# Preparing q, k and v in an attention kernel: the lower parts moved from GpSimd to VectorE, v's bias added by TensorE

## The chip, the cores and the metric

The kernel runs on one core of a Trainium2 chip. The metric is the time on the device of one execution in microseconds (us), lower is better. Engine names are short in the profile: PE is TensorE, PEld its weight loads, DVE is VectorE, ACT is ScalarE, POOL is GpSimd, SP is SyncE.

## What is computed

One transformer layer over 32 sequences of 256 tokens with 128 channels, in float32. The first half is attention with 8 heads:

```python
xn = (x - mu) * rsqrt(var + eps) * gamma + beta      # of an x that was normalised once before
q = xn @ Wq + bq ; k = xn @ Wk + bk                  # 8 heads of 16
v = xn @ Wv + bv                                     # 8 heads of 128
p = softmax(q k^T / 4) ; out = sum over 8 neighbours of (p v)
x = x + out
```

The second half is a mixture of 8 experts with a top-2 choice, `x = x + sum over 2 experts of gate * (gelu(u @ W1 + b1) @ W2 + b2)`, with u the normalised x. The change touches q, k and v only.

Since the output of attention is summed over groups of 8 channels of v, the kernel sums the columns of Wv and bv in such groups once, at the start (`Wv_s`, `bv_s`), and v is then 16 wide for each head.

## The kernel before

Every engine has its own program, written out by hand in the order in which it runs; semaphores (`wait(engine, semaphore, count)`, `.then_inc(...)`) tie them together. Attention is a software pipeline of **periods**, one for each of the 32 sequences (`batch`), with a few before and after. A period of PE has 8 units k = 0 to 7. Unit k holds `max_unit` (L821: two products for the scores' row maxima, of this period's sequence) and `st_unit` (L833: two products for the transposed scores, of the sequence two periods back). Both write PSUM tiles of which there are two, so `max_unit` k waits until DVE has reduced unit k - 2 (`reduce_unit`, L1032), and `st_unit` k until ACT has taken the exponential of unit k - 2 (L682). The products of probabilities and v (`av`, L851) follow at k = 2 and k = 7.

Two sequences form a **pair**, whose normalisation and projections are made together: x is normalised by DVE, POOL and ACT into `z`, transposed by PE and scaled by ACT to `xnT`, and multiplied by Wq at k = 5 of an odd period (L907), by Wk at k = 2 of the next even one (L880), and by `Wv_s` at k = 4 of the even period after that (L931, four products of 128 columns). q and k go through one PSUM tile, `ps_proj`.

The scores need more exactness than one fast product gives, so q and k are each split in a high part (rounded to the type F32R) and a low part, the rest. Before the change this goes as follows for q (k alike, L739, L740 and L554):

```python
act.activation(q_f32[:], ps_proj[:], ACT.Identity, bias=bq_c[:, 0:1])
act.activation(q_hi[par][:], ps_proj[:], ACT.Identity, bias=bq_c[:, 0:1]).then_inc(q_hi_ready, 1)
...
pool.tensor_tensor(lo[par][:], x[:], hi[par][:].bitcast(F32), ALU.subtract).then_inc(lo_ready, 1)
```

ACT copies the projection twice out of PSUM, and POOL subtracts. SP then spreads the parts over `q_stack` and `k_stack` with six DMAs for each sequence (L408), a period before they are needed. v leaves PSUM by DVE (L1173, at k = 6), which adds `bv_s` on the way into `v_aug`.

POOL has a program of its own order in each period (`body` in its block): statistics of the next pair (L578), four indirect DMAs that scatter the rows of `y` to the experts' slots (L590, from period 9 on; each takes POOL's time to issue), the lower part of k (even periods) , the attention output's division and its addition to x (L600, L605), the lower part of q (odd periods), `rstd2` and `shift2` of the second normalisation (L614, L616) for which ACT's copies `y_row` wait (L711), and a piece of splitting the experts' weights (L566, L569). After period 27 DVE builds a table for the experts, and the expert half, with the last periods mixed into it, follows from about 370 us.

## Time and profile before

| what | value |
|---|---|
| median of 3 runs | 707.14 us (706.84 to 707.73) |
| the profiled execution, its own time | 707.2 us |
| its span from first to last instruction | 705.4 us |
| busy: PE, PEld, DVE, ACT, POOL | 578.7, 440.5, 523.7, 486.6, 494.2 us |
| mean granted TensorE clock | 0.937 of full speed |
| share of the chain that ended last: PE, POOL, issue, DMA, DVE, ACT | 38, 20, 9, 6, 6, 4% |

Busy times are sums over engines that work side by side. The chain that ended last follows the work back from the last instruction, at each step to what released it. A timeline shows an engine's instructions with start and length; lengths of neighbours overlap where an engine is pipelined, so what an instruction costs its engine is the distance to the next start. In brackets behind a row stands the engine's idle time before it and what ended that.

### The profile page before, as it was taken

The numbers are of one execution on the slowest core, as the hardware profiler recorded it, in microseconds if no ns is written. First come the engines' busy times: TensorE is split into PE (matmuls) and PEld (weight loads), VectorE is DVE, ScalarE is ACT, GpSimd is POOL, SyncE is SP. The second block draws the span as 40 slices with busy tenths as digits, with TensorE's granted clock in tenths as the row PEclk, the third lists the DMA queues.
The fourth block names the chain that finished last, engine by engine and source line by source line (L and its number), as shares of the span: only waits on it lengthen the run. The fifth ranks groups of instructions, "written<-read, shape, count | busy, mean of one in ns | idle before, by whom it ended". The sixth has DMA issues, their size and how long they took to land.

```text
span 705.4 us, 14432 instructions
## 1 busy us (share of the span) xinstructions
PE 578.7 (82%) x3889; PEld 440.5 (62%) x3889; DVE 523.7 (74%) x1557; ACT 486.6 (69%) x904; POOL 494.2 (70%) x571
## 2 busy tenths in 40 slices
PE   3799998988988989869976888689999999999200
PEld 1566766666666666636644666468888888888200
DVE  7578898988898888888852688457777777777274
ACT  3467878787777787755665887478888888888000
POOL 6434557888888888857886567757788788877700
PEclk9999999999999999979995899899999999999755
DMA  4645545554545645444325567998777778786099
GB/s 118 176 97 153 151 123 159 164 157 136 143 138 162 169 131 155 121 119 121 108 64 163 162 207 212 258 247 263 243 221 246 244 217 246 250 252 198 12 389 324
DMA packets 107570, 127.31 MB, mean 180 GB/s; under 512 B 19950, under 2 KB 86010, under 8 KB 106497
## 3 DMA queue, kind: packets, MB, share of 16 engines
q1 hardware_dynamic: 89600, 105.34, 51.4%
q0 software_dynamic: 9088, 16.94, 7.3%
q10 hardware_dynamic: 8832, 4.46, 2.1%
q8 instruction: 21, 0.34, 0.2%
q14 instruction: 29, 0.23, 0.1%
HBM read 69.26 MB, written 33.72 MB: 146 GB/s over the span
## 4 chain that ended last, share of the span: by engine, by line
PE 38%; POOL 20%; issue 9%; DMA 6%; DVE 6%; ACT 4%; SPq 2%; POOLq 0%; ACTq 0%; DVEq 0%
POOL slots L590 9%; PE ps_max L948 4%; PE ps_max L949 4%; PE ps_max L950 4%; DMA probs<-comb 3%; DMA probs<-slots 3%; PE ps_proj L1001 2%; PE ps_route L993 2%; PE ps_st L948 2%; PE ps_st L949 2%; PE ps_st L950 2%; PE ps_av L851 2%; PE ps_st L833 2%; PE ps_max L821 2%; POOL att_n L600 2%
## 5 line engine op out<-in xcount | busy, mean ns | idle before, releaser
L657 POOL DMA_INDIRECT comb<-probs,gate_row x156 | 179.8, 1152 | 42.9 <-issue 38.9
L1032 DVE TENSOR_REDUCE row_max<-ps_max 128x2 f32<-128x512 f32 x256 | 173.9, 688 | 47.4 <-PE ps_max L821 42.9
L682 ACT ACTIVATE probs<-ps_st 128x512 f32<-128x512 f32 x256 | 146.8, 594 | 57.6 <-PE ps_st L833 55.3
L1257 DVE TENSOR_TENSOR k_stack<-probs,k_stack 128x512 fp32r<-128x512 f32 x156 | 108.1, 693 | 75.1 <-ACT k_stack L783 73.0
L590 POOL DMA_INDIRECT slots<-y_row,slot_idx x128 | 125.5, 980 | 39.2 <-issue 37.6
L821 PE MATMUL ps_max<-k_stack,q_stack 96*128 96x256 f32 x512 | 132.6, 344 | 24.0 <-DVE row_max L1032 22.9
L821 PEld LDWEIGHTS ps_max<-k_stack,q_stack 96*128 96x128 f32 x512 | 81.8, 198 | 71.9 <-DVE row_max L1032 47.0
L833 PE MATMUL ps_st<-q_stack,k_stack 128*128 128x256 f32 x512 | 106.6, 291 | 13.2 <-ACT probs L682 12.8
L833 PEld LDWEIGHTS ps_st<-q_stack,k_stack 128*128 128x128 f32 x512 | 79.6, 192 | 21.3 <-ACT probs L682 19.1
L851 PE MATMUL ps_av<-probs,v_aug 128*32 128x256 f32 x1024 | 70.3, 393 | 0.0
L780 ACT ACTIVATE probs<-ps_st,b_cur 128x512 f32<-128x512 f32 x78 | 53.9, 692 | 23.1 <-DMA b_cur<-b_all 17.5
L948 PE MATMUL ps_max<-k_stack,q_stack 128*128 128x512 f32 x156 | 61.8, 396 | 0.0
L949 PE MATMUL ps_max<-k_stack,q_stack 128*128 128x512 f32 x156 | 61.5, 394 | 0.0
L950 PE MATMUL ps_max<-k_stack,q_stack 128*128 128x512 f32 x156 | 61.4, 394 | 0.0
L783 ACT ACTIVATE k_stack<-ps_st,b_cur 128x512 fp32r<-128x512 f32 x78 | 53.5, 687 | 0.0
L711 ACT ACTIVATE y_row<-X,shift,rstd 128x128 f32<-128x128 f32 (+1 forms) x64 | 27.7, 483 | 25.8 <-POOL shift L616 19.5
L780 ACT ACTIVATE probs<-ps_mv,b_cur 128x512 f32<-128x512 f32 x39 | 26.9, 691 | 21.5 <-PE ps_mv L950 21.0
L851 PEld LDWEIGHTS ps_av<-probs,v_aug 128*32 128x32 f32 x1024 | 27.1, 110 | 19.9 <-issue 1.9
L600 POOL TENSOR_TENSOR att_n<-att,rden 128x256 f32<-128x256 f32 x32 | 21.0, 657 | 22.5 <-DVE rden L1140 22.2
L948 PE MATMUL ps_st<-q_stack 128*128 128x512 f32 x78 | 35.2, 451 | 1.5 <-DVE q_stack L1257 1.5
L1257 DVE TENSOR_TENSOR q_stack<-ps_proj,q_stack 128x512 fp32r<-128x512 f32 x39 | 26.7, 685 | 11.8 <-ACT q_stack L792 11.8
L1001 PE MATMUL ps_proj<-ident,probs 128*128 128x128 f32 x156 | 25.5, 289 | 10.4 <-DMA probs<-slots 10.4
(175 smaller groups left out, 1275.2 us busy)
## 6 DMA issues: line engine op xcount, KB each, us to landing
q_stack<-w_split SPq DMA_DIRECT2D x78, 512.0 KB, 4.3
probs<-slots SPq DMA_DIRECT2D x39, 260.0 KB
q_stack<-q_hi SPq DMA_DIRECT2D x64, 128.0 KB, 2.7
k_stack<-k_hi SPq DMA_DIRECT2D x64, 128.0 KB, 3.0
probs<-comb SPq DMA_DIRECT2D x8, 1024.0 KB, 7.8
X<-in_L_attn_x_dram SPq DMA_DIRECT2D x16, 256.0 KB, 3.3
q_stack<-q_lo SPq DMA_DIRECT2D x32, 128.0 KB, 2.7
k_stack<-k_lo SPq DMA_DIRECT2D x32, 128.0 KB, 3.0
```

What stands on the lines that cost most here:

```text
L590: pool.indirect_dma_start(slots, bass.IndirectOffsetOnAxis(slot_idx[par_s][:, k, c:c + 1], 0), y_row[par_s][k][:, c, :], None).then_inc(sc ...
L657: pool.indirect_dma_start(comb_rows, bass.IndirectOffsetOnAxis(gate_row[r][:, c, 1:2].bitcast(I32), 0), res[r][:, c * P:(c + 1) * P], None ...
L682: act.activation(probs[slot % 2][:, h, :, :], ps_st[h % 2][:], ACT.Exp, scale=DK ** -0.5).then_inc(exp_done, 1)
L780: act.activation(h_f32[f % 2], ps_h[f], ACT.Gelu, bias=b_cur[r][:, f:f + 1]).then_inc(h_f32_ready, 1)
L821: last = pe.matmul(ps_max[k % 2][:, hh, :], q_stack[slot][0:M_ROW, h, sc * P:(sc + 1) * P], k_stack[slot][0:M_ROW, h, :], start=True, stop ...
L833: last = pe.matmul(ps_st[h % 2][:, tc, :], k_stack[slot][:, h, tc * P:(tc + 1) * P], q_stack[slot][:, h, :], start=True, stop=True)
L851: last = pe.matmul(ps_av[32 * j:32 * j + 32, g, :], v_aug[(slot // 2) % 2][:, 2 * (slot % 2) + tc, h, :], probs[slot % 2][:, h, tc, :], st ...
L948: pe.matmul(o, w_hi, x_hi, start=start, stop=False)
L949: pe.matmul(o, w_lo, x_hi, start=False, stop=False)
L950: return pe.matmul(o, w_hi, x_lo, start=False, stop=stop)
L1032: dve.tensor_reduce(row_max[slot % 2][:, sc, 2 * hp:2 * hp + 2], ps_max[k % 2][:], AX.X, ALU.max).then_inc(smax_reduced, 1)
L1257: dve.tensor_tensor(lo, x, hi.bitcast(F32), ALU.subtract).then_inc(s, 1)
```

## The change

ACT no longer writes `q_f32` and `k_f32`. DVE makes the lower parts from PSUM, with one instruction (`proj_lo`): (ps_proj + bias) - high part; for k behind the reduction of unit 4 of an even period, for q behind that of unit 7 of an odd one. POOL's two subtractions go. `ps_proj` is now free only when DVE has read it, so PE's next writers wait for the lower part too. For v, PE first multiplies a row of 128 ones by `bv_s`, repeated four times to 512 columns, and adds the four products with `Wv_s` onto it in PSUM; ACT instead of DVE copies v out, at unit 6.

```diff
             def set_v_and_route():
+                pool.memset(ones_row[:], 1.0).then_inc(v_rest_ready, 1)
...
-                if not t.odd and t.pair(2):
-                    n, par = t.pair(2)
-                    lo_part(n, par, k_f32, k_hi, k_lo, k_hi_ready, k_lo_ready)
...
-                if t.odd and t.pair(3):
-                    n, par = t.pair(3)
-                    lo_part(n, par, q_f32, q_hi, q_lo, q_hi_ready, q_lo_ready)
...
-                        wait(act, k_lo_ready, n)
-                        act.activation(k_f32[:], ps_proj[:], ACT.Identity, bias=bk_c[:, 0:1])
                         act.activation(k_hi[par][:], ps_proj[:], ACT.Identity, bias=bk_c[:, 0:1]).then_inc(k_hi_ready, 1)
...
-                        wait(act, q_lo_ready, n)
-                        act.activation(q_f32[:], ps_proj[:], ACT.Identity, bias=bq_c[:, 0:1])
                         act.activation(q_hi[par][:], ps_proj[:], ACT.Identity, bias=bq_c[:, 0:1]).then_inc(q_hi_ready, 1)
+                    if h == 6 and prep_v:
+                        n, par = prep_v
+                        wait(act, v_proj, n + 1)
+                        wait(act, av_done, 4 * n - 4)
+                        act.activation(v_aug[par][:, :, :, 0:DK], ps_mv[:].rearrange("p (c h d) -> p c h d", c=4, h=H),
+                                       ACT.Copy).then_inc(v_ready, 1)
...
                         wait(pe, q_hi_ready, n + 1)
+                        wait(pe, q_lo_ready, n + 1)
                         pe.matmul(ps_proj[:], Wk_p[:], xnT[par][:], start=True, stop=True).then_inc(k_proj, 1)
...
                         wait(pe, k_hi_ready, n)
+                        wait(pe, k_lo_ready, n)
...
+                        pe.matmul(ps_mv[:], ones_row[:], bv_s[0:1, :].unsqueeze(1).to_broadcast([1, 4, D]), start=True, stop=False)
                         for c in range(4):
                             last = pe.matmul(ps_mv[:, c * P:(c + 1) * P], xnT[par][:, c * P:(c + 1) * P], Wv_s[:],
-                                             start=True, stop=True)
+                                             start=False, stop=(c == 3))
...
+            def proj_lo(n, par, bias, hi, lo, hi_ready, lo_ready):
+
+                wait(dve, hi_ready, n + 1)
+                dve.scalar_tensor_tensor(out=lo[par][:], in0=ps_proj[:], scalar=bias[:, 0:1], in1=hi[par][:].bitcast(F32),
+                                         op0=ALU.add, op1=ALU.subtract).then_inc(lo_ready, 1)
...
+                    if k == 4 and prep_k:
+                        n, par = prep_k
+                        proj_lo(n, par, bk_c, k_hi, k_lo, k_hi_ready, k_lo_ready)
+                    if k == 7 and prep_q:
+                        n, par = prep_q
+                        proj_lo(n, par, bq_c, q_hi, q_lo, q_hi_ready, q_lo_ready)
...
-                    if k == 6 and prep_v:
-                        n, par = prep_v
-                        wait(dve, v_proj, n + 1)
-                        wait(dve, av_done, 4 * n - 4)
-                        dve.tensor_tensor(v_aug[par][:, :, :, 0:DK],
-                                          ps_mv[:].rearrange("p (c h d) -> p c h d", c=4, h=H),
-                                          bv_s[:].rearrange("p (o h d) -> p o h d", o=1, h=H).to_broadcast([P, 4, H, DK]),
-                                          ALU.add).then_inc(v_ready, 1)
```

Three places of the order, by engine. First DVE in an even period, before the change, from the transposition of the attention output at unit 4 to unit 6:

```order
L1136 STREAM_TRANSPOSE att<-ps_av 128x512
L1088 TENSOR_TENSOR y_row_0<-top,gate_rcp 128x4
L1089 TENSOR_SCALAR y_row_0<-token 128x4
L1088 TENSOR_TENSOR y_row_1<-top,gate_rcp 128x4
L1089 TENSOR_SCALAR y_row_1<-token 128x4
L1032 TENSOR_REDUCE row_max<-ps_max 128x2
L1140 RECIPROCAL rden<-att 128x16
L1093 TENSOR_TENSOR token<-token,token_step 128x4
L1095 TENSOR_TENSOR slot_sel<-slot_all,chosen 128x32 x2
L1032 TENSOR_REDUCE row_max<-ps_max 128x2
L1173 TENSOR_TENSOR v_aug<-ps_mv,bv_s 128x32x16
L1103 TENSOR_REDUCE slot_idx<-slot_sel 128x4 x2
```

and the same place now (line numbers are those of the changed kernel):

```order
L1140 STREAM_TRANSPOSE att<-ps_av 128x512
L1035 SCALAR_TENSOR_TENSOR k_lo<-ps_proj,bk_c,k_hi 128x512
L1091 TENSOR_TENSOR y_row_0<-top,gate_rcp 128x4
L1092 TENSOR_SCALAR y_row_0<-token 128x4
L1091 TENSOR_TENSOR y_row_1<-top,gate_rcp 128x4
L1092 TENSOR_SCALAR y_row_1<-token 128x4
L1029 TENSOR_REDUCE row_max<-ps_max 128x2
L1144 RECIPROCAL rden<-att 128x16
L1096 TENSOR_TENSOR token<-token,token_step 128x4
L1098 TENSOR_TENSOR slot_sel<-slot_all,chosen 128x32 x2
L1029 TENSOR_REDUCE row_max<-ps_max 128x2
L1106 TENSOR_REDUCE slot_idx<-slot_sel 128x4 x2
```

The instruction for k's lower part stands ahead of the reduction of unit 5; the one for v, behind the reduction of unit 6, is gone.

Second DVE at the end of an odd period, before:

```order
L1059 MAX_INDEX top_e<-top,sig 128x8 x4
L1032 TENSOR_REDUCE row_max<-ps_max 128x2
L1064 TENSOR_TENSOR chosen<-expert_n,top_e 128x32 x2
L1032 TENSOR_REDUCE row_max<-ps_max 128x2
L1032 TENSOR_REDUCE row_max<-ps_max 128x2
```

and now:

```order
L1062 MAX_INDEX top_e<-top,sig 128x8 x4
L1029 TENSOR_REDUCE row_max<-ps_max 128x2
L1067 TENSOR_TENSOR chosen<-expert_n,top_e 128x32 x2
L1029 TENSOR_REDUCE row_max<-ps_max 128x2
L1035 SCALAR_TENSOR_TENSOR q_lo<-ps_proj,bq_c,q_hi 128x512
L1029 TENSOR_REDUCE row_max<-ps_max 128x2
```

q's lower part stands between the reduction of unit 7 and that of the next period's unit 0.

Third POOL from the scatters of an even period to those of the odd one and on, before:

```order
L588 TENSOR_TENSOR tick<-tick 128x1
L590 DMA slots<-y_row_1,slot_idx 70144x130 x4
L554 TENSOR_TENSOR k_lo<-k_f,k_hi 128x512
L600 TENSOR_TENSOR att_n<-att,rden 128x256
L605 TENSOR_TENSOR X<-X,att_n 128x256
L569 TENSOR_TENSOR w_lo<-Wv_raw,bv_raw 128x512
L588 TENSOR_TENSOR tick<-tick 128x1
L590 DMA slots<-y_row_0,slot_idx 70144x130 x4
L600 TENSOR_TENSOR att_n<-att,rden 128x256
L605 TENSOR_TENSOR X<-X,att_n 128x256
L554 TENSOR_TENSOR q_lo<-q_f,q_hi 128x512
L614 TENSOR_TENSOR rstd<-var,minus_half 128x4
```

and now:

```order
L583 TENSOR_TENSOR tick<-tick 128x1
L585 DMA slots<-y_row_1,slot_idx 70144x130 x4
L592 TENSOR_TENSOR att_n<-att,rden 128x256
L597 TENSOR_TENSOR X<-X,att_n 128x256
L564 TENSOR_TENSOR w_lo<-Wv_raw,bv_raw 128x512
L583 TENSOR_TENSOR tick<-tick 128x1
L585 DMA slots<-y_row_0,slot_idx 70144x130 x4
L592 TENSOR_TENSOR att_n<-att,rden 128x256
L597 TENSOR_TENSOR X<-X,att_n 128x256
L603 TENSOR_TENSOR rstd<-var,minus_half 128x4
```

Both subtractions are gone; nothing else on POOL has moved.

## Rows read from the trace of the kernel before

**Rows 1.** Stretches: length; PE, PEld, DVE, ACT, POOL busy (instructions); clock; DMA share; GB/s.

```profile
42.77:59.87 17.10, 16.31 (x135) 11.67 (x134) 13.06 (x30) 13.75 (x28) 8.42 (x9) 1.00 0.38 112
...
77.30:96.97 19.67, 18.21 (x162) 13.42 (x161) 18.05 (x59) 16.14 (x35) 11.38 (x14) 1.00 0.52 150
96.97:116.30 19.33, 18.43 (x168) 13.69 (x167) 17.86 (x73) 16.22 (x35) 11.50 (x15) 1.00 0.49 144
116.30:137.52 21.22, 18.81 (x168) 13.81 (x167) 18.84 (x73) 16.34 (x35) 18.46 (x23) 1.00 0.52 148
...
266.04:286.91 20.87, 18.89 (x167) 13.77 (x166) 18.60 (x73) 16.23 (x35) 18.09 (x23) 1.00 0.49 142
```

**Rows 2.** Timeline of POOL in one pair: start, length, line, operation, tiles.

```profile
211.53 1.30 POOL L554 TENSOR_TENSOR k_lo<-k_f,k_hi 128x512 fp32r<-128x512 f32 x1
212.77 0.64 POOL L600 TENSOR_TENSOR att_n<-att,rden 128x256 f32<-128x256 f32 x1
...
222.55 1.28 POOL L554 TENSOR_TENSOR q_lo<-q_f,q_hi 128x512 fp32r<-128x512 f32 x1
223.79 1.04 POOL L614 TENSOR_TENSOR rstd<-var,minus_half 128x4 f32<-128x4 f32 x1
```

**Rows 3.** Waits, 150 to 290 us: waiter, releaser, total us, times, longest.

```profile
ACT y_row L711 <- POOL shift L616: 13.2, 7, 2.1
```

**Rows 4.** Timeline of PE, 96.9 to 116.4 us.

```profile
96.97 1.02 PE L880 MATMUL ps_proj<-xnT,Wk_p 128*128 128x512 f32 x2
97.83 0.18 PE L889 MATMUL ps_route<-picked,before 128*128 128x40 bf16 x1
...
99.37 0.40 PE L833 MATMUL ps_st<-q_stack,k_stack 128*128 128x256 f32 x2
99.61 0.40 PE L821 MATMUL ps_max<-k_stack,q_stack 96*128 96x256 f32 x2
99.85 0.40 PE L833 MATMUL ps_st<-q_stack,k_stack 128*128 128x256 f32 x2
100.09 1.05 PE L931 MATMUL ps_mv<-Wv_s,xnT 128*128 128x128 f32 x8
100.89 0.48 PE L821 MATMUL ps_max<-k_stack,q_stack 96*128 96x256 f32 x2
...
102.71 0.50 PE L821 MATMUL ps_max<-k_stack,q_stack 96*128 96x256 f32 x2 [0.19 <-DVE row_max L1032]
...
110.27 1.13 PE L907 MATMUL ps_proj<-xnT,Wq_p 128*128 128x512 f32 x2
...
115.72 0.49 PE L821 MATMUL ps_max<-k_stack,q_stack 96*128 96x256 f32 x2
```

**Rows 5.** Timeline of DVE, the same stretch.

```profile
101.98 0.68 DVE L1032 TENSOR_REDUCE row_max<-ps_max 128x2 f32<-128x512 f32 x1
...
103.56 0.68 DVE L1173 TENSOR_TENSOR v_aug<-ps_mv,bv_s 128x512 f32<-128x512 f32 x1
...
114.28 1.27 DVE L1032 TENSOR_REDUCE row_max<-ps_max 128x2 f32<-128x512 f32 x2
115.48 0.86 DVE L1145 BATCH_NORM_STATS2 bn<-X 128x6 f32<-128x128 f32 x4
```

**Rows 6.** Timeline of ACT, the same stretch.

```profile
99.23 0.66 ACT L739 ACTIVATE k_f<-ps_proj,bk_c 128x512 f32<-128x512 f32 x1
...
102.14 0.59 ACT L760 ACTIVATE yT<-ps_route 128x512 f32<-128x512 f32 x1
```

**Rows 7.** Timeline of all engines, 0 to 46 us.

```profile
10.85 2.88 DVE L1154 TENSOR_SCALAR var_e<-mv 128x4 f32<-128x4 f32 x1
...
28.75 1.91 PE L931 MATMUL ps_mv<-Wv_s,xnT 128*128 128x128 f32 x8
```

**Rows 8.** Timeline of PE, 300 to 345 us.

```profile
302.16 1.02 PE L907 MATMUL ps_proj<-xnT,Wq_p 128*128 128x512 f32 x2
...
319.80 1.05 PE L931 MATMUL ps_mv<-Wv_s,xnT 128*128 128x128 f32 x8
```

More of the change, by code:

```diff
@@ L69, in build @@
         k_lo = [sb(f"k_lo{n}", [P, 512], F32R) for n in range(2)]
-        q_f32 = sb("q_f32", [P, 512])
-        k_f32 = sb("k_f32", [P, 512])
         xnT = [sb(f"xnT{n}", [P, 512]) for n in range(2)]
@@ L97, in build @@
         bv_s = sb("bv_s", [P, D])
+        ones_row = sb("ones_row", [1, P])
         bq_c = sb("bq_c", [P, 1])
@@ L549, in set_v_and_route @@
                 pool.memset(pad_rows[:, :, D + 1].bitcast(I32), 2 * TOP_K * ROWS).then_inc(route_const, 1)
-            def lo_part(n, par, x, hi, lo, hi_ready, lo_ready):
-                wait(pool, hi_ready, n + 1)
-                pool.tensor_tensor(lo[par][:], x[:], hi[par][:].bitcast(F32), ALU.subtract).then_inc(lo_ready, 1)
             def by_part(w, which):
@@ L687, in body @@
                 prep_k = None if t.odd else t.pair(2)
+                prep_v = None if t.odd else t.pair(0)
                 ry = None if t.odd else t.pair(-6)
@@ L843, in av @@
                         if t.fixed and b == 0:
-                            pe.wait_ge(v_rest_ready, 2)
+                            pe.wait_ge(v_rest_ready, 3)
                         wait(pe, v_ready, n + 1)
@@ L927, in body @@
                             pe.wait_ge(wv_ready, 2)
+                            pe.wait_ge(v_rest_ready, 3)
                         if t.batch(1):
                             wait(pe, neg_maxT_ready, t.batch(1)[0] + 1)
+                        pe.matmul(ps_mv[:], ones_row[:], bv_s[0:1, :].unsqueeze(1).to_broadcast([1, 4, D]), start=True, stop=False)
                         for c in range(4):
                             last = pe.matmul(ps_mv[:, c * P:(c + 1) * P], xnT[par][:, c * P:(c + 1) * P], Wv_s[:],
-                                             start=True, stop=True)
+                                             start=False, stop=(c == 3))
                         last.then_inc(v_proj, 1)
@@ L944, in _ @@
             pe.wait_ge(k_hi_ready, B // 2)
+            pe.wait_ge(k_lo_ready, B // 2)
             def three(o, w_hi, w_lo, x_hi, x_lo, start, stop):
@@ L1108, in body @@
                 ln2 = t.pair(-5) if t.odd else None
-                prep_v = None if t.odd else t.pair(0)
+                prep_q = t.pair(3) if t.odd else None
+                prep_k = None if t.odd else t.pair(2)
                 chn = t.pair(-7) if t.odd else None
```

## The prediction

> **What bounds the kernel now.** I read four views: busy times over stretches, the waits, the chain, then single timelines. The expert half, from some 370 us on, has no instruction of the change, so all of it happens before. I cut that part at PE's product for k (L880), once per pair of periods. The stretches show three regimes [rows 1]. Early, 17.1 us a pair, PE is busy for 16.3 of them: PE is the bound. From 77 us DVE has grown to 17.9 to 18.1 busy, as the choice of experts joins, and a pair takes 19.7 and 19.3 us with POOL at 11.5. From 116 us the scatters have joined and POOL is busy for 18.1 to 18.5 us, to which the time in which it issues its scatters has to be added: its timeline has no gap but those. From 116.30 to 286.91 there are 8 pairs, 170.6 us, 21.33 each: POOL is the bound, and ACT waits up to 2.1 us for its `shift2` [rows 3]. So two prices are needed: POOL's work off a pair that POOL bounds, and PE's and DVE's work onto a pair of 19.33 us, which is what the same work takes when POOL does not bind.
>
> **POOL's relief.** k's lower part holds POOL from 211.53 to 212.77, 1.24 us, and q's from 222.55 to 223.79, 1.24 [rows 2]. A POOL-bound pair would go from 21.33 to 18.85 us. That is under 19.33, so POOL stops being the bound and PE and DVE decide.
>
> **PE's new product.** It streams 512 columns of float32 with one row of weights. The nearest rows: the product for k, also 512 columns, takes 0.86 us to the next start (96.97 to 97.83), and v's four products of 128 columns 0.80 (100.09 to 100.89) [rows 4]. Could one row be cheaper than 128? `ps_max` with 96 rows and `ps_st` with 128 rows take the same 0.24 us from start to start for the same columns (99.37, 99.61, 99.85) [rows 4], so rows seem not to matter; the bounds are 0 and 0.86, I take 0.86, since the k product has the same columns and type. The Trainium skill (TensorE: Matmul & The Clock Gate, "Why this matters for your kernels") states that a single product with 32 rows lasts as long as one with 128; by it this product has no discount either, and no run here shows one row yet.
>
> **DVE.** It loses v's addition and gains two instructions, which like it read 512 float32 from PSUM and as many from SBUF and write as many. v's addition lasts 0.68 us, about 0.60 to the next start [rows 5]. So DVE has +0.60 a pair net, but not where it was: I walk the pair of 19.33 us.
> - Even period. DVE is late there: PE's product at 102.71 waits for the reduction that starts at 101.98 [rows 4, 5]. k's lower part goes ahead of that reduction: +0.60. PE's extra 0.86 falls between 100.09 and that same wait, so it lies beside the 0.60; PE idled 0.19 before the product, which leaves 0.67. The later of the two counts: +0.65. v's addition goes away behind it, where PE did not wait: nothing.
> - Odd period. q's lower part goes between two reductions that run without a gap (114.28 on, with the statistics at 115.48 right behind) [rows 5]. The first product that needs the later one starts at 115.72, 0.17 us after that reduction ended (114.28 + 1.27 = 115.55) [rows 4, 5]: +0.60 - 0.17, so +0.45 rounded.
>
> A pair becomes 19.33 + 0.65 + 0.45 = 20.4; I add 0.1 for small DVE instructions that run slower beside a busy POOL, and take **20.5 us** against 21.33. Bounds: 19.33 (all hidden) and 21.33 (nothing gained).
>
> **ACT** loses two copies (0.66 us each) and gains one like `yT`'s, 0.59 [rows 6]. It has 16.2 us of work in 19.3, so this costs nothing; should ACT bind, it is a gain of up to 0.7. The added semaphore waits of PE on `q_lo` and `k_lo` sit at k = 2 and k = 3 of the next period, several units behind DVE's instruction; if DVE were later than that, PE would stop with everything behind it. SP's DMAs wait for `q_lo` and `k_lo` a period later; they come earlier than from POOL.
>
> **The sum**, against the profiled execution's 707.2 us (its span is 705.4; the median of the runs, 707.14, is the same time to 0.1):
> - Start: v's first product lasts 1.91 us where it lasts 1.05 later [rows 4, 7], so the new one costs about 0.86 x 2 = 1.7. k's first lower part comes earlier, by about 0.6 and ACT's copy 0.6, but DVE's first reductions must now wait for the second q: I take -0.8, bounds 0 and -1.8. Together +0.9.
> - Two PE-bound pairs (42.77 to 77.30; the first stands in the rows): +0.86 each, +1.7. Third: +0.86 + 0.45 = +1.3. Fourth: +0.65 + 0.45 = +1.1.
> - Eight pairs from 116.30: 8 x (20.5 - 21.33) = -6.6.
> - 286.91 to the next product for q at 302.16, 15.25 us, still POOL's; the same piece of the unbound pair is 96.97 to 110.27, 13.3 [rows 1, 4, 8]. With +0.65 and 0.2 for the busy POOL, 14.15: -1.1.
> - End: the last q, +0.45; the last two products for v (319.80 and one 18 us later) [rows 8], at full speed, 0.86 each, of which 0.2 hides behind POOL: +1.5.
>
> +0.9 + 1.7 + 1.3 + 1.1 - 6.6 - 1.1 + 0.45 + 1.5 = -0.8. **706.4 us**: what POOL gives back in the middle is paid for at both ends and by PE and DVE. A measurement of this kernel can tell about 0.2%, 1.4 us, from no change: under 705.7 or over 708.6.
>
> **Rivals.**
> - *DVE gets back more than it is given.* In the pair without scatters the same 73 instructions keep DVE busy 17.86 us, in POOL-bound ones 18.84 and 18.60 [rows 1], and a 4-column instruction at 10.85 us lasted 2.88 while POOL filled k's stacks [rows 7]. If much of this difference of some 0.9 comes from POOL's two subtractions, a pair is 0.6 shorter than I took: 8 x -0.6 = -4.8, 701.6 us. Against it: most of POOL's time is scatters, and they stay. The Trainium skill (GPSIMD Engine Reference, "Specifications") says that GpSimd shares SBUF interfaces with VectorE, and contends with its two-port modes or two SBUF inputs; by that rule the new instructions, with one input in PSUM, are not slowed, and this rival's gain is real. The rows on DVE's busy time go its way, without telling which POOL instruction is to blame.
> - *PE and DVE add up (the other side).* If PE's 0.86 and DVE's additions do not overlap, because a late `ps_max` makes DVE late and DVE in turn the next `ps_max`, the pair grows by 0.86 + 0.68 = 1.54, to 20.9. Against my forecast that is 8 x +0.4 = +3.2, for the third and fourth pair +0.7 together, for the last piece +0.3: 710.6 us. It decides once the pair passes 20.7. For it: DVE and PE have 1.5 and 0.9 us of idle time left in the pair of 19.33, so both are near full.
> - *The change does not free the middle.* Another wait holds the pair at 21.33, such as PE's new wait on `k_lo` or `q_lo`, or ACT's on `shift2`. Then the middle gives nothing: 706.4 + 6.6 + 1.1 = 714.1.
>
> **Chances and range.** My forecast 0.45, its own range 704.0 to 708.9 (faster 0.13, same 0.23, slower 0.09); DVE's relief 0.28, faster; adding up 0.22, slower; middle not freed 0.05, slower. Faster 0.41, same 0.23, slower 0.36. The range takes in both main rivals: 700.5 to 711.5.
>
> **What would show it.** POOL has idle time before its scatters from 116 us on, and ACT's wait on `shift2` shrinks. The new product takes 0.8 to 0.9 us to the next start. The two DVE instructions last 0.68. Pairs: 18.0 early, 20.5 in the middle. I am wrong if the middle pairs stay over 21 or fall under 20, if the one-row product is cheap, or if the early pairs do not grow: then PE was not their bound.

## The result and the profile after

The changed kernel takes 711.54 us (median of 8 runs, 707.38 to 714.48), the kernel before on the same chip 707.19 (8 runs, 706.81 to 707.98). The ratio is 1.0054, 95% interval 1.0036 to 1.0072: slower, by about 0.5%. The profiled execution of the changed kernel is the shortest of its eight, 707.38 us with a span of 705.6; so the trace explains a difference of 0.2 us from the profiled execution before, and the median lies 4.2 us above what the trace shows. One execution in experiment 1 took 1049.35 us at a mean granted clock of 0.61; it stands in its median, 710.25 (709.97 without it), and in no ratio.

Stretches of the changed kernel, again from one product for k to the next; the columns are those of [rows 1]:

```profile
45.48:63.78 18.30, 17.54 (x136) 12.04 (x135) 13.87 (x31) 12.85 (x26) 5.03 (x6) 1.00 0.36 105
...
82.48:103.35 20.87, 19.56 (x165) 13.70 (x164) 17.56 (x59) 16.05 (x35) 7.58 (x10) 1.00 0.51 142
103.35:124.03 20.68, 19.66 (x169) 13.96 (x168) 18.60 (x73) 15.11 (x32) 10.60 (x14) 1.00 0.48 142
...
206.88:227.32 20.44, 19.70 (x170) 13.97 (x169) 18.35 (x73) 15.63 (x33) 16.24 (x21) 1.00 0.53 155
268.23:288.56 20.33, 19.68 (x169) 13.98 (x168) 18.24 (x73) 15.57 (x33) 15.74 (x21) 1.00 0.50 145
```

Beside [rows 1], the first early pair went from 17.10 to 18.30 us, the third and fourth from 19.67 and 19.33 to 20.87 and 20.68. The eight middle pairs together went from 170.6 to 164.5 us (124.03 to 288.56), 20.57 each where they took 21.33. In these eight POOL is busy for 15.7 to 16.3 us where it was for 17.6 to 18.6, PE for 19.7 to 20.0 where it was for 18.7 to 18.9. The first product for k of the row comes at 45.48 us instead of 42.77. The account from one profiled execution to the other: start +2.7, four early pairs +1.20, +1.27, +1.20 and +1.35, eight middle pairs -6.1, everything behind the last of them -1.45 (705.6 - 288.56 = 417.0 against 705.4 - 286.91 = 418.5). The sum is +0.2.

The timeline of PE around the new product in an early pair (start, length, line, operation, tiles), and below it that of its weight loads (PEld):

```profile
66.55 0.40 PE L825 MATMUL ps_st<-q_stack,k_stack 128*128 128x256 f32 x2
66.88 1.12 PE L925 MATMUL ps_mv<-bv_s,ones_row 1*128 1x512 f32 x2
67.94 1.16 PE L927 MATMUL ps_mv<-Wv_s,xnT 128*128 128x128 f32 x8
68.85 0.48 PE L813 MATMUL ps_max<-k_stack,q_stack 96*128 96x256 f32 x2
```

```profile
66.43 0.31 PEld L825 LDWEIGHTS ps_st<-q_stack,k_stack 128*128 128x128 f32 x2
66.88 0.29 PEld L925 LDWEIGHTS ps_mv<-bv_s,ones_row 1*128 1x128 f32 x2
67.93 0.97 PEld L927 LDWEIGHTS ps_mv<-Wv_s,xnT 128*128 128x128 f32 x8 [0.76 <-issue]
```

From one product to the next stand 0.33 us before the new one (its neighbours take 0.24), 1.06 for itself and 0.91 for v's (0.80 before [rows 4]). The detour, the product with what it adds ahead of it and behind it, costs 0.09 + 1.06 + 0.11 = 1.26 us, not 0.86. The loads differ in the same places: `ps_st`'s weights start at 66.43, 0.12 us ahead of its product, but the new product's load starts with the product, and v's weights are not loaded while it runs; they start with v's product.

At the start, where PE's products take twice as long (by their durations the lower of its two clock levels, 1.2 for 2.4 GHz) until about 41 us, the new one costs 2.0 us and v's 1.73:

```profile
27.19 1.94 PE L813 MATMUL ps_max<-k_stack,q_stack 96*128 96x256 f32 x4
29.05 2.07 PE L925 MATMUL ps_mv<-bv_s,ones_row 1*128 1x512 f32 x2
31.05 2.08 PE L927 MATMUL ps_mv<-Wv_s,xnT 128*128 128x128 f32 x8
32.78 0.77 PE L813 MATMUL ps_max<-k_stack,q_stack 96*128 96x256 f32 x2
```

DVE's new instructions, one in each period, and their neighbours, then ACT's copy of v:

```profile
211.01 0.71 DVE L1140 STREAM_TRANSPOSE att<-ps_av 128x512 f32<-128x512 f32 x1
211.64 0.71 DVE L1035 SCALAR_TENSOR_TENSOR k_lo<-ps_proj,bk_c,k_hi 128x512 fp32r<-128x512 f32 x1
212.27 0.15 DVE L1091 TENSOR_TENSOR y_row<-top,gate_rcp 128x4 f32<-128x4 f32 x1
...
225.34 0.74 DVE L1035 SCALAR_TENSOR_TENSOR q_lo<-ps_proj,bq_c,q_hi 128x512 fp32r<-128x512 f32 x1
226.00 0.68 DVE L1029 TENSOR_REDUCE row_max<-ps_max 128x2 f32<-128x512 f32 x1
```

```profile
214.26 0.62 ACT L747 ACTIVATE v_aug<-ps_mv 128x512 f32<-128x512 f32 x1
```

They last 0.71 and 0.74 us and take 0.63 and 0.66 of DVE's time to the next start. POOL now waits for others before it scatters, and ACT's wait for POOL's `shift` between 150 and 290 us fell from 13.2 us [rows 3] to 6.1 (timeline of POOL, then the row of the waits):

```profile
216.89 1.55 POOL L564 TENSOR_TENSOR w_lo<-Wv_raw,bv_raw 128x512 fp32r<-128x512 f32 x1
219.09 0.22 POOL L583 TENSOR_TENSOR tick<-tick 128x1 f32<-128x1 f32 x1 [0.65 <-PE ps_av L843]
```

```profile
ACT y_row L701 <- POOL shift L605: 6.1, 7, 1.0
```

### The profile page after: what moved, and what is told of

Its sections match the earlier page's. It is cut to its first block, busy times and chain, and to the rows that moved or that the text cites. A ratio compares the mean times of both kernels' runs of the same rounds, so it can differ in the third digit from the quotient of the medians.

```text
span 705.6 us, 14453 instructions
## 1 busy us (share of the span) xinstructions
PE 594.9 (84%) x3921; PEld 443.8 (63%) x3921; DVE 526.7 (75%) x1573; ACT 476.1 (67%) x888; POOL 459.4 (65%) x540
## 4 chain that ended last, share of the span: by engine, by line
PE 34%; DMA 6%; DVE 4%; POOL 4%; issue 3%; ACT 3%; SPq 2%; POOLq 0%; ACTq 0%; DVEq 0%
PE ps_max L945 4%; PE ps_max L946 4%; PE ps_max L947 4%; DMA probs<-comb 3%; PE ps_proj L998 2%; DMA probs<-slots 2%; PE ps_route L990 2%; PE ps_st L945 2%; PE ps_st L946 2%; PE ps_st L947 2%; POOL comb L646 1%; PE ps_mv L945 1%; PE ps_mv L947 1%; PE ps_mv L946 1%; POOL slots L585 1%
## 5 line engine op out<-in xcount | busy, mean ns | idle before, releaser
L646 POOL DMA_INDIRECT comb<-probs,gate_row x156 | 182.3, 1168 | 42.8 <-issue 39.0
L813 PE MATMUL ps_max<-k_stack,q_stack 96*128 96x256 f32 x512 | 130.8, 340 | 19.5 <-DVE row_max L1029 18.2
L825 PE MATMUL ps_st<-q_stack,k_stack 128*128 128x256 f32 x512 | 104.6, 287 | 1.8 <-ACT probs L671 1.5
L772 ACT ACTIVATE probs<-ps_st,b_cur 128x512 f32<-128x512 f32 x78 | 53.9, 691 | 20.1 <-DMA b_cur<-b_all 13.6
L573 POOL TENSOR_TENSOR rstd<-var_e,minus_half 128x4 f32<-128x4 f32 x16 | 16.2, 1011 | 42.6 <-DVE var_e L1164 42.6
L772 ACT ACTIVATE probs<-ps_mv,b_cur 128x512 f32<-128x512 f32 x39 | 26.9, 691 | 23.2 <-PE ps_mv L947 23.1
L843 PEld LDWEIGHTS ps_av<-probs,v_aug 128*32 128x32 f32 x1024 | 27.1, 110 | 19.7 <-issue 1.4
```

The source lines that it names most:

```text
L646: pool.indirect_dma_start(comb_rows, bass.IndirectOffsetOnAxis(gate_row[r][:, c, 1:2].bitcast(I32), 0), res[r][:, c * P:(c + 1) * P], None ...
L772: act.activation(h_f32[f % 2], ps_h[f], ACT.Gelu, bias=b_cur[r][:, f:f + 1]).then_inc(h_f32_ready, 1)
L813: last = pe.matmul(ps_max[k % 2][:, hh, :], q_stack[slot][0:M_ROW, h, sc * P:(sc + 1) * P], k_stack[slot][0:M_ROW, h, :], start=True, stop ...
L825: last = pe.matmul(ps_st[h % 2][:, tc, :], k_stack[slot][:, h, tc * P:(tc + 1) * P], q_stack[slot][:, h, :], start=True, stop=True)
L843: last = pe.matmul(ps_av[32 * j:32 * j + 32, g, :], v_aug[(slot // 2) % 2][:, 2 * (slot % 2) + tc, h, :], probs[slot % 2][:, h, tc, :], st ...
```

## The experiments

All of them were profiled. The table gives, for each trace, the start of the product for k that opens the row of pairs, the first, second and fourth pair, the mean of the eight middle pairs and the time from the last of them to the end of the span, in us, then the median of the runs and the ratio to the kernel before on the same chip with its interval. Experiments 1 to 4 shared a chip, and so did 5 to 8. Experiments 9 to 13 all name the same third chip, which had changed between 11 and 12: its median for the kernel before was 758.11 us beside 9 to 11 and 709.13 beside 12 and 13.

| kernel | first K | pair 1 | pair 2 | pair 4 | middle | rest | median | ratio |
|---|---|---|---|---|---|---|---|---|
| before | 42.77 | 17.10 | 17.43 | 19.33 | 21.33 | 418.5 | 707.19 | 1 |
| changed | 45.48 | 18.30 | 18.70 | 20.68 | 20.57 | 417.0 | 711.54 | 1.0054 |
| 1 changed, again | 45.51 | 18.28 | 18.69 | 20.67 | 20.56 | 419.7 | 710.25 | 1.0027 (1.0004-1.0049) |
| 2 lower parts only | 41.12 | 17.02 | 18.06 | 20.50 | 20.45 | 418.4 | 701.96 | 0.9925 (0.9899-0.9951) |
| 3 v only | 44.93 | 18.31 | 18.69 | 20.13 | 21.74 | 422.4 | 721.57 | 1.0200 (1.0174-1.0225) |
| 4 product over 128 rows | 41.19 | 17.87 | 18.32 | 20.51 | 20.45 | 419.7 | 703.30 | 0.9942 (0.9922-0.9963) |
| 5 only the first over 128 | 41.25 | 18.31 | 18.68 | 20.68 | 20.82 | 419.2 | 707.91 | 1.0020 (0.9995-1.0046) |
| 6 only the first over 1 | 45.60 | 17.91 | 18.30 | 20.52 | 20.53 | 417.1 | 707.19 | 0.9995 (0.9978-1.0011) |
| 7 no bias product | 43.41 | 16.69 | 18.04 | 20.53 | 20.46 | 418.1 | 701.99 | 0.9921 (0.9899-0.9942) |
| 8 before, again | 43.95 | 16.74 | 17.44 | 19.32 | 21.34 | 419.4 | 708.93 (one) | |
| 9 over 32 rows | 45.07 | 18.30 | 18.70 | 20.67 | 22.15 | 453.5 | see below | |
| 10 over 64 rows | 45.53 | 18.27 | 18.68 | 20.70 | 22.11 | 470.4 | see below | |
| 11 k's lower part only | 42.42 | 17.35 | 18.06 | 20.54 | 21.79 | 451.2 | see below | |
| 12 the same, again | 41.73 | 17.38 | 18.03 | 19.97 | 20.23 | 419.2 | 700.49 | 0.9882 (0.9864-0.9900) |
| 13 lower parts only, again | 40.84 | 17.05 | 18.05 | 20.51 | 20.68 | 417.8 | 702.62 | 0.9919 (0.9898-0.9940) |

### 1. The changed kernel again

No edit.

> The changed kernel once more, for its spread (707.4 to 714.5 us in eight executions, while the kernel before stays within 1.2 us) and for a second trace. Theory A (TensorE's clock): the executions differ in when the granted clock rises at the start or falls later; a trace of a slower execution then shows the first product for k at full speed (1.02 us) later than the 45.5 us of the first trace, or more time at the half clock (mean granted clock under 0.94), and middle pairs of the same 20.4 to 20.5 us. Theory B (the pipeline itself): the middle pairs are longer in slower executions, 20.7 us and more, at the same clock. Median expected 711 us by both.

710.25 us, on this chip 0.27% over the kernel before. Its trace repeats that of the changed kernel to 0.04 us at every product for k from 45.5 to 288.5 us; the profiled execution took 709.97 us, and the 2.6 us over the first all lie behind 288.5. So the start of 45.5 and the pairs come again with the kernel, and the part behind them, mostly the expert half, which has no instruction of the change, differs by 2 to 3 us from execution to execution. Over all traces but those of experiments 3 and 9 to 11 the rest behind the pairs lies between 417.0 and 419.7 us.

### 2 and 3. Each half of the change alone

Experiment 2 keeps q's and k's lower parts on DVE and leaves v as before; experiment 3 is the reverse.

```diff
-pe.matmul(ps_mv[:], ones_row[:], bv_s[0:1, :].unsqueeze(1).to_broadcast([1, 4, D]), start=True, stop=False)
...
-act.activation(v_aug[par][:, :, :, 0:DK], ps_mv[:].rearrange("p (c h d) -> p c h d", c=4, h=H),
-               ACT.Copy).then_inc(v_ready, 1)
...
+dve.tensor_tensor(v_aug[par][:, :, :, 0:DK],
+                  ps_mv[:].rearrange("p (c h d) -> p c h d", c=4, h=H),
+                  bv_s[:].rearrange("p (o h d) -> p o h d", o=1, h=H).to_broadcast([P, 4, H, DK]),
+                  ALU.add).then_inc(v_ready, 1)
```

The edit of 2 against the changed kernel is above; with the product gone, the four products with `Wv_s` begin a new sum again (`start=True`). The edit of 3 against the kernel before is the same with its signs turned round, and brings `ones_row` and the waits for it.

> Half of the change: lower parts by DVE, v as before (bias added by DVE on the way out of PSUM, no product with ones). Theory 1 (the new product on PE is what eats the gain): early pairs back at 17.1 to 17.4 us, middle pairs 20.0 to 20.4, 698 to 701 us. Rival (DVE was the bound in the middle): with v's addition back on DVE the middle pairs are 20.8 us or more, 703 to 706 us. Spread: if it comes from the product at the start it goes, if from DVE's waits at the start it stays.

> The other half: the product with ones on PE and ACT's copy of v, lower parts by ACT and POOL as before. Theory 1: POOL still bounds the middle (21.3 us a pair), where PE has room; the start and the early pairs pay 1.25 us each for the product, so 707 + 2.5 (start) + 4 x 1.2 + 2 x 1.2 = 716 us. Rival (the product hides beside DVE): 708 to 710 us. Spread: present if the product brings it.

2 measured 0.75% faster than the kernel before, 3 measured 2.0% slower. The lower parts bring 6.0 us, v's part alone costs 13.6 and on top of the lower parts 710.25 - 701.96 = 8.3. In 2 the first pair takes 17.02 us, as in the kernel before (17.10), and a middle pair 20.45, near the changed kernel's 20.57: the whole gain of the middle belongs to the lower parts. 3 is 5.6 us over its expectation of 716. In it POOL keeps its subtractions and stays the bound (18.1 us busy and its issues, as in [rows 1]); a middle pair in which the clock stayed at 1.00 took this:

```profile
144.05:165.27 21.22, 19.97 (x169) 14.17 (x168) 17.71 (x72) 16.77 (x36) 18.06 (x23) 1.00 0.56 161
```

Of the 13.6 us, 2.2 lie at the start, 4.4 in the four early pairs, 3.3 in the middle (in three pairs the clock fell to 0.92) and 3.9 behind; the dips and the part behind were not in the expectation.

### 4. The product over 128 rows instead of one

```diff
-ones_row = sb("ones_row", [1, P])
+ones_row = sb("ones_row", [P, P])
-pool.memset(ones_row[:], 1.0).then_inc(v_rest_ready, 1)
+pool.memset(ones_row[:], 1.0 / P).then_inc(v_rest_ready, 1)
-pe.matmul(ps_mv[:], ones_row[:], bv_s[0:1, :].unsqueeze(1).to_broadcast([1, 4, D]), start=True, stop=False)
+pe.matmul(ps_mv[:], ones_row[:], bv_s[:].unsqueeze(1).to_broadcast([P, 4, D]), start=True, stop=False)
```

> The changed kernel with the product over 128 rows (a 128 x 128 matrix of 1/128, and the bias on every partition) instead of one row, the same 512 columns. Theory 1 (a product with one row costs more than one with 128, since the array changes its row group before and after it): 0.86 us to the next start instead of 1.06, v's products 0.80 instead of 0.91, early pairs 18.3 instead of 18.7 us, 3 to 5 us less in all, 707 to 708 us. Rival (the cost is that of an accumulation onto the same tile or of 512 columns as such): nothing changes, 711 us.

703.30 us, ratio 0.9942: the change becomes faster than the kernel before by one edit that gives PE 128 times as many multiplications. That is some 4 us under the expectation, which had the price of the product right and nothing for the start. Timeline of PE and of its weight loads, the same place of the program as above:

```profile
61.83 0.40 PE L825 MATMUL ps_st<-q_stack,k_stack 128*128 128x256 f32 x2
62.07 1.02 PE L925 MATMUL ps_mv<-bv_s,ones_row 128*128 128x512 f32 x2
62.93 1.05 PE L927 MATMUL ps_mv<-Wv_s,xnT 128*128 128x128 f32 x8
63.74 0.49 PE L813 MATMUL ps_max<-k_stack,q_stack 96*128 96x256 f32 x2
```

```profile
61.95 0.31 PEld L925 LDWEIGHTS ps_mv<-bv_s,ones_row 128*128 128x128 f32 x2
62.50 0.19 PEld L927 LDWEIGHTS ps_mv<-Wv_s,xnT 128*128 128x128 f32 x1 [0.24 <-issue]
62.93 0.86 PEld L927 LDWEIGHTS ps_mv<-Wv_s,xnT 128*128 128x128 f32 x7 [0.24 <-issue]
```

0.24 us before the product, 0.86 for it, 0.81 for v's: exactly the price of the prediction. Its load starts 0.12 us ahead of it, v's first load 0.43 us ahead of v's product. With one row the detour costs 0.40 us more. Up to the end of the middle the kernel is 288.52 - 281.96 = 6.6 us ahead of experiment 1: 4.3 at the start, 0.4 in each of the first three pairs, 0.2 in the fourth and 0.9 in the middle. At the start the same step falls on the place where the products become short:

```profile
28.80 1.09 PE L925 MATMUL ps_mv<-bv_s,ones_row 128*128 128x512 f32 x2
29.73 1.05 PE L927 MATMUL ps_mv<-Wv_s,xnT 128*128 128x128 f32 x8
```

### 5 and 6. One row and 128 rows, divided between the start and the rest

```diff
+if t.fixed and n == 0:
+    pe.matmul(ps_mv[:], ones_all[:], bv_s[:].unsqueeze(1).to_broadcast([P, 4, D]), start=True, stop=False)
+else:
     pe.matmul(ps_mv[:], ones_row[:], bv_s[0:1, :].unsqueeze(1).to_broadcast([1, 4, D]), start=True, stop=False)
```

That is 5, with `ones_all` 128 rows of 1/128 (one more fill on POOL at the start, in both); in 6 the condition is `not (t.fixed and n == 0)`.

> The changed kernel, but its very first bias product (batch element 0, at about 29 us) contracts over 128 rows; the other thirteen stay at one row. Theory 'the form of the first product delays the start': the K products start near 41.2 us instead of 45.5, and the time is that of the kernel with all products over 128 rows plus the 2.5 us of the later pairs, 705.8. Rival 'the start is the chance of one execution, or is set by all the products': the start stays at 45.5 and the time near 710. Theory 'size of the product in each pair': early pairs stay at 18.3 and 18.7.

> The mirror: only the first bias product has one row, the other thirteen contract over 128 rows. Theory 'the form of the first product delays the start': K products start near 45.5 us, the early pairs take 17.9 and 18.3, and the time is near 707.5. Rival 'chance of one execution': start at 41.2 or at 45.5 whatever the form, and a time near 703.5.

The traces did what the theory said, 41.25 and 45.60 at the start, 18.31 and 17.91 in the first pair. 6 came out at 707.19 us, as expected, 5 at 707.91, 2 us above its expectation. Its trace shows one place where such a difference can come from: in one middle pair the clock fell.

```profile
119.78:142.44 22.66, 21.62 (x170) 15.63 (x168) 19.44 (x73) 15.80 (x33) 16.20 (x21) 0.92 0.47 135
142.44:163.34 20.90, 19.96 (x169) 14.02 (x168) 19.12 (x73) 15.75 (x33) 15.68 (x21) 1.00 0.55 158
```

At a granted clock of 0.92 the pair takes 22.66 us, 1.6 more than the 21.0 of the same pair in the changed kernel. 6 and 4 differ in the first product (and the fill), and their intervals lie apart (0.9978 to 1.0011, 0.9922 to 0.9963): 3.9 us for one instruction at 29 us (on two chips, whose medians of the kernel before are 707.25 and 707.93). 5 and 1 differ by the same edit, and their intervals overlap: in the times the gain is shown by one of the two comparisons only, in the traces by both.

### 7. Without the bias product

```diff
-pe.matmul(ps_mv[:], ones_row[:], bv_s[0:1, :].unsqueeze(1).to_broadcast([1, 4, D]), start=True, stop=False)
```

The four products with `Wv_s` begin the sum (`start=True`). This kernel leaves out v's bias, so its result is not the layer's; it prices the product.

> The changed kernel without the bias product: v's bias is left out of the computation, ACT copies v as before. It prices the product as a whole. If TensorE's row of work sets the early pairs, they fall from 18.3 and 18.7 to about 17.1 and 17.4, as in the kernel before; the middle pairs fall from 20.57 to 20.0 if the product is on their path, or stay near 20.4 if VectorE's 18.4 us of work and its waits set them. Time 698 to 701.

701.99 us, 8.3 us below experiment 1 and level with experiment 2. The second pair (18.04, not the 17.4 of the expectation), the fourth (20.53) and the middle (20.46) are those of experiment 2; the third is longer, 20.12 against 19.77. So moving v's evacuation between DVE and ACT is worth nothing that shows in the time, and the middle does not feel the product either, since at 128 rows it is 20.45 and without it 20.46. The rival of the expectation holds there. But DVE is not full (18.25 us of 20.31), nor is any other engine; what makes 20.4 us out of 18.7 of PE and 18.3 of DVE was not taken apart further.

This run also limits the theory about the start. Up to v's first product its timeline of PE is that of experiment 13, and yet it is still slow there (7 first, then 13):

```profile
28.80 1.91 PE L926 MATMUL ps_mv<-Wv_s,xnT 128*128 128x128 f32 x8
30.37 0.92 PE L813 MATMUL ps_max<-k_stack,q_stack 96*128 96x256 f32 x4
```

```profile
28.82 1.23 PE L920 MATMUL ps_mv<-Wv_s,xnT 128*128 128x128 f32 x8
29.80 0.72 PE L807 MATMUL ps_max<-k_stack,q_stack 96*128 96x256 f32 x4
```

The record of the granted clock reads 1.00 in this stretch for both, so it does not show the difference; the steps of 1.57 and 0.98 us do. But 7 was not slow for long: a little later its products are short, and from 34 us the record itself falls to 0.50 and stays there until 44 (one row of the timeline, one of the stretches):

```profile
31.83 0.50 PE L813 MATMUL ps_max<-k_stack,q_stack 96*128 96x256 f32 x2 [0.54 <-DVE row_max L1028]
```

```profile
36.00:44.00 8.00, 7.54 (x26) 5.53 (x25) 5.77 (x18) 3.26 (x6) 0.00 (x0) 0.50 0.25 59
```

Experiment 8 did the same (0.50 from 34.7 to 44.9 us) and 12 for a shorter time (35 to 38.4). All six traces with few rows in the first product (changed, 1, 3, 6, 9, 10) stayed slow until about 41 us, with a record of 1.00 throughout, and had their first K at 44.9 to 45.6. Of the five others in which DVE makes both lower parts, four (2, 4, 5, 13) became fast at 29 us and had it at 40.8 to 41.3. So the start has two ways of losing time, products that stay long under a record of 1.00 and a fall of the record to 0.50. The first goes with the few rows in every trace; why it does, and when the second comes, stays open.

### 8. The kernel before again

No edit, one run.

> The kernel before, unchanged, for a second trace. Theory 'the expert half differs from execution to execution': K products start where they did in the first trace (42.77, 59.87, 77.30 us and so on), and the difference in time lies behind 310 us. Rival 'the start differs from execution to execution': the first K product starts at another time, 41 or 45 us.

708.93 us for this execution. The start is 1.2 us later than in the first trace, with the clock at half in part of it, the pairs agree within 0.1 us from the second on apart from single ones of up to 1, and the rest takes 419.4 instead of 418.5. Both theories of the expectation have a share.

### 9 and 10. The product over 32 and over 64 rows

The edit of experiment 4 with 32 and 64 in place of P, and `bv_s[0:32, :]` and `bv_s[0:64, :]`.

> The changed kernel with the bias products over 32 rows of 1/32. In the traces so far the product over one row takes a step of 1.06 us and 0.34 us stand before it, with its weight load starting together with it and not 0.12 us ahead; over 128 rows the step is 0.86 us and the loads run ahead. Theory 'below some number of rows no weight load overlaps with products of full height': 32 rows behave like one row (step 1.06, next v step 0.91, early pairs 18.3 and 18.7) or like 128 (0.86; 17.9 and 18.3), not between. Rival 'the cost grows as the rows get fewer': a step between 0.86 and 1.06. Start: if few rows delay it, 45.5 us with 32 rows too, time near 710; if only a single row does, 41.2 and 703.5.

> The same over 64 rows of 1/64. Theory 'a number of rows decides': 64 rows behave either as one row (near 710) or as 128 rows (near 703.5), and with the run over 32 rows this says on which side of which number. Rival 'gradual': a step of the product between that over 32 and that over 128 rows, and a time between.

The times say nothing about the rows: this chip ran the kernel before at a median of 758.11 us (745.5 to 768.58); 9 took 770.76 (ratio 1.0346, 1.0238 to 1.0454), 10 took 769.23 (1.0247, 1.0179 to 1.0315). In their traces the middle pairs are long, some with a stretch at half clock and some almost without (22.56 us at 0.99), and the rest behind them takes 453.5 and 470.4 us; what disturbed this chip is not shown. The early pairs were undisturbed, and they answer the question (9, then 10; timelines of PE):

```profile
66.47 1.12 PE L925 MATMUL ps_mv<-bv_s,ones_row 32*128 32x512 f32 x2
67.52 1.16 PE L927 MATMUL ps_mv<-Wv_s,xnT 128*128 128x128 f32 x8
68.44 0.48 PE L813 MATMUL ps_max<-k_stack,q_stack 96*128 96x256 f32 x2
```

```profile
66.91 1.12 PE L925 MATMUL ps_mv<-bv_s,ones_row 64*128 64x512 f32 x2
67.96 1.16 PE L927 MATMUL ps_mv<-Wv_s,xnT 128*128 128x128 f32 x8
68.87 0.48 PE L813 MATMUL ps_max<-k_stack,q_stack 96*128 96x256 f32 x2
```

32 and 64 rows cost what one row costs: 1.05 us and 0.92 or 0.91 behind it, loads that start with their product, pairs of 18.30 and 18.70. Below 64 rows the price does not grow as rows get fewer. `ps_max` with its 96 rows, beside `ps_st` with 128, takes 0.24 us [rows 4], and its weights load 0.12 us ahead (99.49 and 99.61 us in the kernel before). But `q_stack` and `k_stack` are of the type F32R, and these two products of 256 columns take together less than a third of what 512 columns of float32 take. So 1, 32 and 64 rows of float32 are of one kind here and 128 of the other. The limit lies between 64 and 128, and at most at 96 only if the type makes no difference, which no run tested.

### 11, 12 and 13. How much of POOL's relief is needed

11 and 12 are experiment 2 with q's lower part left to ACT's copy and POOL's subtraction, as before; 13 is experiment 2 once more.

```diff
+act.activation(q_f32[:], ps_proj[:], ACT.Identity, bias=bq_c[:, 0:1])
...
+pool.tensor_tensor(q_lo[par][:], q_f32[:], q_hi[par][:].bitcast(F32), ALU.subtract).then_inc(q_lo_ready, 1)
...
-proj_lo(n, par, bq_c, q_hi, q_lo, q_hi_ready, q_lo_ready)
```

> Of the change only k's lower part moves to VectorE; q's stays with ACT and GpSimd, and v's bias is added as before. It halves the move. Theory 'GpSimd's row of work sets the middle pairs only while it is longer than about 20.4 us': one subtraction of 1.24 us less takes the pair from 21.33 to 20.4 at once, and the time is that of the kernel with both lower parts on VectorE, 702, or below it by up to 2 where VectorE's second instruction costs the early pairs. Rival 'each subtraction gives its own half': middle pairs near 20.9 and a time of 704 to 705.

> Only k's lower part on VectorE, once more on a chip in its usual condition, beside the kernel with both lower parts moved. Theory 'the middle pair is set by GpSimd only while its work is over 20.4 us': middle pairs near 20.4, a time of 700 to 702. Rival 'each subtraction gives its own half': middle pairs near 20.9, 704 to 705.

> Both lower parts on VectorE, v's bias as before, once more. From its first trace: K products start at 41.1 or 42.8 to 44 us by how the granted clock rises at the start, early pairs 17.0 and 18.1, middle pairs 20.3 to 20.5, a time near 702 and 0.7% below the kernel before. If its gain came only from the early rise of the clock in one execution, the time is 704 or more.

11 ran beside 9 and 10, on the chip as it then was (758.84 us against 758.11; the ratio on record is 1.0173, 1.0092 to 1.0255), where its own middle pairs took 20.8 to 23.2 us, three of them with stretches at half clock; it tells nothing about the question. 12 measured 700.49 us beside 709.13 before, ratio 0.9882; 13 measured 702.62, as expected, with the middle pairs 0.2 above the expectation. Stretches of 12, the fourth pair and the last middle pair, then the same of experiment 2:

```profile
97.15:117.12 19.97, 18.47 (x167) 13.74 (x166) 18.49 (x74) 15.66 (x34) 10.23 (x14) 1.00 0.48 139
...
259.04:278.97 19.93, 18.91 (x167) 13.79 (x166) 18.82 (x74) 15.64 (x34) 16.86 (x22) 1.00 0.50 148
```

```profile
95.97:116.47 20.50, 18.67 (x167) 13.67 (x166) 19.11 (x74) 14.72 (x31) 10.56 (x14) 1.00 0.49 143
...
259.86:280.03 20.17, 18.71 (x168) 13.71 (x167) 19.22 (x74) 15.04 (x32) 15.16 (x20) 1.00 0.49 143
```

One subtraction less on POOL is enough. The middle pair is 20.23 us with one moved (20.9 if each subtraction gave its own half) and 20.45 and 20.68 with both. The last two are the same kernel, both at a clock of 1.00, so a difference of 0.2 between such means is not a result. Nor is the fourth pair, which POOL never bounded: it takes 19.97 us in 12 and 20.50 with both moved, but 20.54 in 11, the same kernel as 12, at a clock of 1.00. This version beats the kernel before, and its median is the lowest of all. That it beats the one with both moved is likely, not certain: beside it on the same chip their intervals just touch (0.9864 to 0.9900, 0.9898 to 0.9940).

## Why the prediction was wrong

Forecast were 706.4 us, 700.5 to 711.5; measured 711.54. The step that failed is the price of PE's new product: with the product that costs what was priced (experiment 4) the time is 703.30 us, inside the range, and with the one of the change it is 710.25 on the same chip, 7 us more. By the prediction's own steps:

- **PE's new product, the step that failed.** It said that "rows seem not to matter; the bounds are 0 and 0.86, I take 0.86". Rows do matter: with 1, 32 or 64 the detour costs 1.26 us, 0.40 above the upper bound. The bounds came from products with 96 and 128 rows only, and the comparison of those two from products of another type (F32R); they could not enclose a float32 product with a single row. A price taken from so far had to reach above 0.86 as well as below. The Trainium skill (TensorE: Matmul & The Clock Gate, "Why this matters for your kernels"), which says that a single product with 32 rows lasts as long as one with 128, does not hold between products of full height in this kernel: experiment 9 shows 1.05 us for 32 rows, experiment 4 0.86 for 128.
- **The start, +0.9, was +2.7.** The product took 2.0 us there and not 1.7, v's 1.73 where it had taken 1.57, and PE stayed slow some 12 us longer than where the product over 128 rows stood in its place (experiments 4 and 6, 3.9 us in the medians). That the form of this product goes with when the products become short was in no term and no rival. It is the larger part of the 7 us: 4.3 of the 6.6 that the traces of 1 and 4 show up to the end of the middle.
- **Early pairs.** Forecast +0.86, +0.86, +1.3, +1.1; measured +1.20, +1.27, +1.20, +1.35. In the first pair the product is the whole of it (experiment 2: -0.08 without it). In the second 0.6 of it is DVE's lower part for k (experiment 2: 18.06 against 17.43; experiment 12, with k's alone, 18.03), which the prediction had put at nothing. In the third the product is the larger part (19.77 in experiment 2, 20.47 with it over 128 rows, 20.87 with one). In the fourth DVE's additions count and the product lies beside them as forecast: without it 20.53, with it over 128 rows 20.51, with one row 20.67.
- **POOL stops being the bound, a pair of 20.5.** Right: 20.57, and 20.45 without the excess of one row. But the gain is not of the whole move: half of it gives at least as much (20.23, experiment 12).
- **The middle, -6.6, was -6.1**; the last piece to the product for q, -1.1, was -0.5 (288.56 to 303.35, 14.8 us).
- **The end, +1.95 in its two terms, was about +0.6** up to the last product of attention (65.5 us behind the product for q before, 66.1 now), and the expert half behind it, which the forecast left alone, was 1.5 us shorter in this execution. In experiment 1 the same part took some 2 us more.
- **DVE's instructions at 0.68** were 0.71 and 0.74, with steps of 0.63 and 0.66 where 0.60 was taken: 0.1 a pair, as much as was added for a busy POOL.
- **The rivals.** "DVE gets back more than it is given" had the mechanism right and its value wrong: from the third middle pair on DVE is busy for 18.3 us on average with 0.77 us of new work in it, where it was busy for 18.5 without (17.9 to 18.9). So it did get back the 0.9 us of the rival, and yet the pair stayed at 20.4, not 19.9. "PE and DVE add up" asked for pairs of 20.9, which only the first two middle pairs reached (21.0 and 20.9). That the change doesn't free the middle was wrong.
- **The rest of the miss.** Against the profiled execution the forecast is off by 1.0 us, and that is luck: up to the product for q the measured terms lie 3.9 us above the forecast ones, and the 2.9 us at the end and in the expert half that go the other way hide it. Experiment 4 says the same from the other side: with the product at the forecast price the time is 3.1 us under the forecast, 2.5 of it at the start. The median is off by 5.1. The other seven executions of the changed kernel have no trace. Three sources of such a difference are shown: the rest behind the pairs (up to 2.7 us), a dip of the clock in a middle pair (1.6 us), and middle pairs that are longer at a clock of 1.00 (experiments 2 and 13, the same kernel, 1.9 us over the eight). That they also make up those 4.2 us is likely, but not shown, nor is why the runs of the kernel before lay closer together that time.

## What to carry to other kernels

A product with few rows is not a cheap one: before a bias is added by a row of ones between products of full height, try the same product over 128 rows of 1/128, or leave the bias where it was. Take from the bounding engine only what makes it stop being the bound; here the second piece of work moved cost its new engine and bought nothing. And where an operation has no row of its kind in the trace, rows of another kind (fewer rows, another type) give its price no upper bound.

## What the runs showed of the hardware

- Products over 1, 32 and 64 rows between products over 128 cost 1.26 us (experiments 1, 9 and 10) where 128 rows cost 0.86 (experiment 4; 512 columns of float32 at full clock), and neither their weights nor v's behind them load ahead. That the loads are the cause was not tested apart.
- The form of one product at 29 us goes with 3.9 us: PE becomes fast there or some 12 us later. With few rows it never did so early (six traces), with 128 always (two), without the product in two of three; the third was fast a little later and fell back to a granted clock of 0.50.
- Small DVE instructions with two inputs in SBUF can last until a POOL instruction with two inputs of 512 elements ends. Groups by line, in the kernel before between 202 and 287 us, then in the changed kernel between 207 and 289 us (the second number is the mean in ns):

```profile
L1074 DVE TENSOR_TENSOR picked<-chosen 128x32 bf16<-128x32 f32 x5 | 2.7, 546 | 0.0
L1049 DVE TENSOR_TENSOR den<-expn,ones 128x32 f32<-128x32 f32 x4 | 1.8, 442 | 0.0
```

```profile
L1077 DVE TENSOR_TENSOR picked<-chosen 128x32 bf16<-128x32 f32 x4 | 0.7, 176 | 0.0
L1052 DVE TENSOR_TENSOR den<-expn,ones 128x32 f32<-128x32 f32 x4 | 0.7, 173 | 0.0
```

  In experiment 12, which keeps POOL's subtraction for q, the timelines of DVE and POOL show one such wait; the two end together, at 198.69 and 198.65:

```profile
197.91 0.78 DVE L1076 TENSOR_TENSOR picked<-chosen 128x32 bf16<-128x32 f32 x1
```

```profile
197.38 1.27 POOL L603 TENSOR_TENSOR q_lo<-q_f,q_hi 128x512 fp32r<-128x512 f32 x1
```

  The reductions from PSUM do not stretch (685 ns in the kernel before, 687 in the changed one). The Trainium skill (GPSIMD Engine Reference, "Specifications") says that the two engines contend where VectorE has two inputs in SBUF; the trace agrees with it for these instructions, which have two, and for the reductions, which have none.
